# Output buffer freed at the head of a GpSimd step, and row loads awaited two units later on a semaphore for each parity

## The chip, the cores and the metric

The kernel runs on one core of a Trainium2 chip. The metric is device time in microseconds (us) of one execution; the number compared is the median over several runs. Lower is better. The core's engines are TensorE (PE), VectorE (DVE), ScalarE (ACT), GpSimd (POOL) and SyncE (SP), which work in parallel and are tied together by semaphores; 16 DMA engines move data between HBM and the core's memory.

## What is computed

Eight blocks of 100 tokens of width 512 go through an attention-like layer (keys, gate and values are the same context `c`) and then through a top-1 mixture of 16 experts. Cut to what matters:

```python
x = x + einsum(gelu(layernorm(x) @ c.T) * (layernorm(x) @ c.T), c)     # per block, c is 722 x 512
h = layernorm(x).reshape(800, 512)
logits = h @ router_w                     # 512 x 16
assign = argmax(logits); w = sigmoid(logits[assign])
out = (gelu(h @ w1[assign] + b1[assign]) @ w2[assign] + b2[assign]) * w
x = x + out
```

Each expert has `w1` (512 x 1024) and `w2` (1024 x 512) in f32, so 4 MB; all 16 are read once.

## The kernel before

**First part, to about 120 us.** For each of the eight blocks PE, ACT and DVE compute the first layer, the routing and each token's rank in its expert. Rows (token, gate, mean, inverse root, output row number) are scattered by GpSimd into a table `rows` in HBM, sorted by expert.

**Second part, in units.** A unit is up to 32 tokens of one expert. A unit's rows are laid as 128 partitions x 132 values (4 quarters of the token's width). Units 0 to 3 are head units of experts 0 to 3; all further ones stand in the order of the experts, and with the inputs drawn there are 32 units in all (the trace has 32 scatters at L860). By a count of the tokens that these inputs send to each expert, units 8 to 11 belong to expert 3, unit 12 to expert 4, units 28 to 30 to expert 14 and unit 31 to expert 15.

For unit j the engines do:

- PE: `first_layer(j)` (L385, into `p_h`), the transpose of the next unit's tokens (L404), `second_layer(j-1)` (L396, into `p_y`). `second_layer(j)` waits until `finish(j-1)` has read `p_y` (`s_yo`).
- DVE: transpose and bias of the hidden units (L682, L688), normalization of the tokens two units ahead (`next_tokens(j+2)`, L672, which waits on `s_land` for the rows to have landed), bias of the residual (L694), and `finish(j-1)` (L705), which writes one half of the double buffer `y_out`. `finish(j)` waits on `s_y_free >= j + 1`.
- ACT: the gelu (L491).
- GpSimd: `scatter_unit(j, r)`, with r the parity of j: it waits until scatter j-2, which read the same half of `y_out`, has landed (`s_done[r]`), adds one to `s_y_free`, copies the row numbers (L856), waits for `finish(j)` (`s_yo`) and issues the indirect DMA to `out` (L860). While rows are still to be loaded, GpSimd also issues two row loads per unit (`load_unit`, L213, 66 KB each; each first reads its column from a table into a register, L212).
- SP: `load_half` (L232), 1 MB pieces of the experts' weights, four to an expert. There are four slots of weights; experts 4 to 15 (48 pieces) go into a slot when the expert four before has done its last `first_layer` (`s_hp`, for w1) or `second_layer` (`s_y`, for w2). The pieces are issued in order.

**What sets the order on GpSimd.** All is written out by hand, each engine's instructions run in program order. Units 8 to 11 are loaded beside `scatter_unit(2)` and `(3)`. Then a loop L888 of `loading` rounds (4 here) takes two units a round: `scatter_unit(4)` to `(11)`, with the loads of units 12 to 27. A loop L895 loads the units left over (28 to 31), after which the last wait on `s_ld` stands, and a loop L899 runs `scatter_unit(12)` to `(31)` with no loads. All row loads from unit 8 on count on the one semaphore `s_ld`; GpSimd tells DVE of landed rows by `s_land`. The step of a unit in L888 is: issue two loads, wait `s_next` and `s_done[r]`, free `y_out`, scatter, then wait on `s_ld` for the loads issued in this same step.

Of the kernel before, what the change touches and what calls it, by code (L numbers as in the profile page):

```python
# [35 lines left out]
SLOTS = 4  # L36
# [3 lines left out]
OWN = 8  # L40
NEAR = 12
# [47 lines left out]
def build(nc, x, ctx_main, ctx_rest, ctxT_a, ctxT_b, router, w1, b1, w2, b2, consts, out):  # L89
# [3 lines left out]
    with ExitStack() as stack:  # L93
# [3 lines left out]
        def sem(name):  # L97
            return stack.enter_context(nc.semaphore(name))

        def sems(name, n):  # L100
            return [sem(f"{name}{i}") for i in range(n)]
# [75 lines left out]
        s_x, s_ctx = sems("s_x_in", 3), sems("s_ctx", 2)  # L177
        s_w1, s_w2 = ([sems(f"{n}_{i}_", 2) for i in range(SLOTS)] for n in ("s_w1", "s_w2"))
        s_b2, s_b2_rest, s_row = sem("s_b2"), sem("s_b2_rest"), sems("s_row", RB)
        s_own, s_ld, s_land, s_blank = sems("s_own", OWN - SLOTS), sem("s_ld"), sem("s_land"), sem("s_blank")  # L180

        s_x1ps, s_tps, s_lgps = sems("s_x1ps", 2), sem("s_tps"), sem("s_lgps")
        s_xnps, s_att, s_rkps, s_cntps = sem("s_xnps"), sem("s_att"), sem("s_rkps"), sem("s_cntps")
# [16 lines left out]
        s_next = sem("s_next")  # L200
        s_prep, s_yo, s_out_at, s_y_free = (sem(n) for n in ("s_prep", "s_yo", "s_out_at", "s_y_free"))
# [5 lines left out]
        def units(eng):  # L207
            return eng.value_load(ends[0:1, E - 1:E], min_val=SLOTS + E, max_val=MAXU)

        def load_unit(eng, j, signal):  # L210
            at = bass.ds(j, 1) if not isinstance(j, int) else slice(j, j + 1)
            col = eng.value_load(colof[0:1, at], min_val=0, max_val=E * PER - 1)  # L212
            eng.dma_start(xr[:, at, :].rearrange("p o d -> p (o d)"),  # L213
                          rows[bass.ds(col * U, U), :].rearrange("t (q d) -> q t d", q=Q)).then_inc(signal, 16)
# [571 lines left out]
        def _(pool):  # L786
            def apart():
                pool.sem_inc(s_apart_p, 1)
# [55 lines left out]
                                             nothing[:, :], None, bounds_check=last_row, oob_is_err=False  # L844
                                             ).then_inc(s_pad[i], 16)

            def scatter_unit(j, r, before):
                at = slice(j, j + 1) if isinstance(j, int) else bass.ds(j, 1)
                mine = head if isinstance(j, int) and j < SLOTS else xr
                pool.wait_ge(s_next, j + 1)  # L850
                if before is not None:
                    pool.wait_ge(s_done[r], before)
                apart()
                if before is not None:
                    pool.sem_inc(s_y_free, 1)  # L855
                nc.gpsimd.tensor_copy(out_at[r][:, :], mine[:, at, DQ + 3].bitcast(U32)).then_inc(s_out_at, 1)  # L856
                pool.wait_ge(s_out_at, j + 1)
                pool.wait_ge(s_yo, j + 3)
                apart()
                nc.gpsimd.indirect_dma_start(out_q, bass.IndirectOffsetOnAxis(ap=out_at[r][:, :], axis=0),  # L860
                                             y_out[:, r, :], None, bounds_check=last_out, oob_is_err=False
                                             ).then_inc(s_done[r], 16)

            scatter_unit(0, 0, None)
            pool.wait_ge(s_blank, 1)
            for i in range(RB):
# [5 lines left out]
            for j in range(SLOTS + 1, OWN):  # L872
                load_unit(pool, j, s_own[j - SLOTS])
            scatter_unit(1, 1, None)
            for i in range(1, PADS):
                pool.wait_ge(s_pad[i], 16)
                apart()

            for j in range(2, SLOTS):
                for k in range(2):  # L880
                    load_unit(pool, OWN + 2 * (j - 2) + k, s_ld)
                scatter_unit(j, j % 2, 16 * (j // 2))
                pool.wait_ge(s_ld, 32 * (j - 1))
                pool.sem_inc(s_land, 2)
            n = units(pool)
            less = pool.value_load(n_less[0:1, 0:1], min_val=SLOTS + E - NEAR - 1, max_val=MAXU - NEAR - 1)
            loading, pairs = pool.snap(less // 4), pool.snap((less + (NEAR - 2)) // 2)
            with pool.Fori(0, loading) as i:  # L888
                for r in range(2):
                    for k in range(2):  # L890
                        load_unit(pool, 4 * i + (NEAR + 2 * r + k), s_ld)
                    scatter_unit(2 * i + (SLOTS + r), r, 16 * i + 32)
                    pool.wait_ge(s_ld, 64 * i + (16 * (NEAR - OWN) + 32 * r + 32))
                    pool.sem_inc(s_land, 2)
            with pool.Fori(4 * loading + NEAR, n) as j:  # L895
                load_unit(pool, j, s_ld)
            pool.wait_ge(s_ld, 16 * less + 16 * (NEAR + 1 - OWN))
            pool.sem_inc(s_land, 4)
            with pool.Fori(loading, pairs) as i:  # L899
                for r in range(2):  # L900
# [36 lines left out]
```

## Time and profile before

| | us |
|---|---|
| median of 3 runs (lowest to highest) | 328.78 (328.36 to 329.91) |
| the profiled execution, its own time | 326.27 |
| its span in the profile | 324.6 |
| granted TensorE clock, mean over the span | 0.911 |
| busy: PE / PE weight load / DVE / POOL / ACT | 253.4 / 179.8 / 113.0 / 89.0 / 32.4 |

The numbers of the trace are those of the profiled execution: 1.67 us of its time lie outside the span, and it is 2.5 us below the median of the runs. A row of the timeline is start, duration, engine, line, operation, and in brackets how long the engine had been idle and what ended that. The weights and activations have come from one queue that SP issues (q1), the row loads and scatters from one that GpSimd issues (q0).

### The profile page before, as it was taken

To read this page: it belongs to the slowest core of one execution; us is meant where nothing else is said; L and a number is where in the kernel's file an instruction comes from. 1 tells how busy PE (TensorE), PEld (TensorE's weight loads), DVE (VectorE), ACT (ScalarE), POOL (GpSimd) and SP (SyncE) were. 2 spreads that over 40 slices of the span, in tenths; PEclk is the share of its full clock that TensorE was granted. 3 is DMA by queue.
4 is the path that set the end of the run, shared out by engine and by line. 5 is a ranking of instruction groups with operands and counts; after the bars stand their busy time and mean duration, and the time that the engine had idled before them with its cause. 6 is when DMAs were issued, how large, how long until landed. Compare 5 with 4: busy or idle time off the path is not lost. (4 is left out here: it accounts for less than half of the span.)

```text
span 324.6 us, 9969 instructions
## 1 busy us (share of the span) xinstructions
PE 253.4 (78%) x3763; PEld 179.8 (55%) x3764; DVE 113.0 (35%) x385; ACT 32.4 (10%) x76; POOL 89.0 (27%) x141
## 2 busy tenths in 40 slices
PE   1899999999999898784663747840197999899982
PEld 0868867867867456553431544520175766566762
DVE  2134444444442663242210222220043344344430
ACT  0311111112011021010000000000010111011110
POOL 1002312312341353533330234413022122221222
PEclk9999999999999959995979569895579999999998
DMA  7999899999999998753999806599759999999700
GB/s 252 377 357 361 287 371 343 385 378 342 418 381 309 420 418 327 121 182 138 291 403 361 305 25 236 176 364 375 245 209 424 424 423 426 420 421 424 289 16 14
DMA packets 21437, 100.93 MB, mean 311 GB/s; under 512 B 4942, under 2 KB 6882, under 8 KB 12200
## 3 DMA queue, kind: packets, MB, share of 16 engines
q1 hardware_dynamic: 16680, 93.81, 77.0%
q0 software_dynamic: 4592, 6.56, 6.6%
q8 instruction: 14, 0.23, 0.3%
q10 hardware_dynamic: 144, 0.27, 0.2%
q14 instruction: 7, 0.06, 0.1%
HBM read 95.89 MB, written 5.14 MB: 311 GB/s over the span
## 5 line engine op out<-in xcount | busy, mean ns | idle before, releaser
L396 PE MATMUL bank<-W,area 128*32 128x128 f32 x2048 | 76.2, 295 | 41.3 <-DVE area L705 38.5
L396 PEld LDWEIGHTS bank<-W,area 128*32 128x32 f32 x2048 | 61.9, 118 | 51.5 <-DVE area L705 40.3
L385 PE MATMUL bank<-W,area 128*32 128x256 f32 x1024 | 69.0, 409 | 14.9 <-issue 14.5
L385 PEld LDWEIGHTS bank<-W,area 128*32 128x32 f32 x1024 | 37.1, 117 | 36.8 <-issue 24.6
L860 POOL DMA_INDIRECT out<-area,out_at x32 | 32.4, 1012 | 72.1 <-DVE area L705 57.8
L316 PEld LDWEIGHTS bank<-xnT,area 128*128 128x128 f32 (+1 forms) x384 | 44.7, 194 | 4.7 <-issue 4.7
L323 PE MATMUL bank<-area,hidT 128*100 128x512 f32 (+1 forms) x96 | 46.8, 601 | 0.0
L316 PE MATMUL bank<-xnT,area 128*128 128x100 f32 (+1 forms) x384 | 45.1, 280 | 1.4 <-issue 1.4
L705 DVE SCALAR_TENSOR_TENSOR area<-bank,area 128x128 f32 (+1 forms) x28 | 9.8, 351 | 86.7 <-POOLq L855 65.8
L213 POOL DMA_DIRECT2D area<-rows x27 | 19.2, 711 | 53.5 <-issue 53.5
L491 ACT ACTIVATE area<-area 128x256 f32<-128x256 f32 x32 | 13.4, 417 | 187.6 <-PE bank L396 177.5
L682 DVE STREAM_TRANSPOSE area<-bank 128x256 f32<-128x256 f32 x32 | 14.4, 449 | 39.6 <-PE bank L385 28.4
L804 POOL DMA_INDIRECT rows<-row,pos x8 | 8.7, 1082 | 49.6 <-DVE pos L569 32.6
L323 PEld LDWEIGHTS bank<-area,hidT 128*100 128x100 f32 (+1 forms) x96 | 13.7, 167 | 10.0 <-issue 10.0
L525 DVE TENSOR_TENSOR hidT<-hidT,bank 128x300 f32<-128x300 f32 x16 | 7.4, 464 | 19.5 <-ACT hidT L463 19.5
L688 DVE TENSOR_TENSOR area<-area,b1s 128x256 f32<-128x256 f32 x32 | 13.6, 424 | 0.2 <-DVE area L682 0.2
L404 PEld LDWEIGHTS bank<-con,area 128*128 128x128 f32 x33 | 4.7, 142 | 14.7 <-issue 14.6
L672 DVE TENSOR_SCALAR area<-area 128x128 f32 (+1 forms) x28 | 9.8, 350 | 7.7 <-DMA area<-rows 3.9
L463 ACT ACTIVATE hidT<-bank 128x300 f32<-128x300 f32 x16 | 6.8, 422 | 56.4 <-PE bank L316 56.4
L792 POOL TENSOR_TENSOR rs_x<-ve_x,con 100x1 f32<-100x1 f32 x8 | 4.5, 558 | 25.9 <-DVE ve_x L511 25.9
L404 PE MATMUL bank<-con,area 128*128 128x128 f32 x33 | 11.2, 341 | 0.1
L792 POOL TENSOR_TENSOR row<-ve_t,con 100x4 f32<-100x4 f32 x8 | 8.4, 1049 | 9.2 <-DVE ve_t L511 9.0
(95 smaller groups left out, 146.0 us busy)
## 6 DMA issues: line engine op xcount, KB each, us to landing
W<-in_w SPq DMA_DIRECT2D x64, 1024.0 KB, 11.9
area<-in_ctx_main SPq DMA_DIRECT2D x8, 1280.0 KB
area<-in_ctxT_a SPq DMA_DIRECT2D x8, 768.0 KB, 8.8
area<-in_ctxT_b SPq DMA_DIRECT2D x8, 676.0 KB, 8.0
area<-rows POOLq DMA_DIRECT2D x27, 66.0 KB, 7.1
xs<-in_x SPq DMA_DIRECT2D x8, 200.0 KB
area<-in_ctx_rest SPq DMA_DIRECT2D x8, 160.0 KB
xs<-in_b SPq DMA_DIRECT2D x4, 192.0 KB
```

Source lines behind the costliest of these rows:

```text
L213: eng.dma_start(xr[:, at, :].rearrange("p o d -> p (o d)"), rows[bass.ds(col * U, U), :].rearrange("t (q d) -> q t d", q=Q)).then_inc(sign ...
L316: last = nc.tensor.matmul((p_xa, p_xb)[part][0:n, T * c:T * c + T], ctxTs[b % 2][part][:, k, P * c:P * c + n], xnT[:, k, :], start=(k == 0 ...
L323: last = nc.tensor.matmul(p_att[0:T, :], hidT[0:CW[c], c, :], cxs[b % 2][0:CW[c], c, :], start=(c == 0), stop=(c == SC - 1))
L385: last = nc.tensor.matmul(p_h[U * q:U * q + U, 0:FQ], curT[:, U * k:U * k + U], mine, start=(k == 0), stop=(k == KD - 1), tile_position=(0 ...
L396: last = nc.tensor.matmul(p_y[U * q:U * q + U, 0:DQ], hT[:, U * c:U * c + U], W2[:, slot, c, DQ * q:DQ * q + DQ], start=(c == 0), stop=(c ...
L404: nc.tensor.transpose(p_blk[:, 0:P], cur, ident).then_inc(s_blk, 1)
L491: nc.scalar.activation(hT, h_pre, ACT.Gelu).then_inc(s_act, 1)
L672: nc.vector.tensor_scalar(cur, mine[:, 0:DQ], mine[:, DQ + 1:DQ + 2], mine[:, DQ + 2:DQ + 3], ALU.subtract, ALU.mult).then_inc(s_next, 1)
L682: nc.vector.transpose(h_pre, p_h[:, 0:FQ]).then_inc(s_hT, 1)
L688: nc.vector.tensor_tensor(view, view, bias.unsqueeze(3).to_broadcast([P, 2, Q, U]), ALU.add).then_inc(s_hb, 1)
L792: nc.gpsimd.tensor_tensor(rs, ve, neg_half.to_broadcast(list(rs.shape)), ALU.pow).then_inc(s_rs, 1)
L860: nc.gpsimd.indirect_dma_start(out_q, bass.IndirectOffsetOnAxis(ap=out_at[r][:, :], axis=0), y_out[:, r, :], None, bounds_check=last_out, ...
```

## The change

Line numbers in the text are those of the kernel before. In `scatter_unit`, the wait for scatter j-2 and the increment of `s_y_free` now come first; then an optional hook runs, then the wait on `s_next`, the copy, the wait on `s_yo` and the scatter, as before. The hook is `load_two`: it waits for the pair of loads issued two units ago (the one of the same parity, on its own semaphore `s_ld[r]`), adds 2 to `s_land`, and issues the next two loads. The loads left over count on a third semaphore, `s_left`. After them GpSimd waits for both parities and then for `s_left`, before `scatter_unit(12)`.

```diff
-            def scatter_unit(j, r, before):
+            def scatter_unit(j, r, before, ahead=None):
                 at = slice(j, j + 1) if isinstance(j, int) else bass.ds(j, 1)
                 mine = head if isinstance(j, int) and j < SLOTS else xr
-                pool.wait_ge(s_next, j + 1)
                 if before is not None:
                     pool.wait_ge(s_done[r], before)
+                    apart()
+                    pool.sem_inc(s_y_free, 1)
+                if ahead is not None:
+                    ahead()
+                pool.wait_ge(s_next, j + 1)
                 apart()
-                if before is not None:
-                    pool.sem_inc(s_y_free, 1)
                 nc.gpsimd.tensor_copy(out_at[r][:, :], mine[:, at, DQ + 3].bitcast(U32)).then_inc(s_out_at, 1)
...
-            for j in range(2, SLOTS):
+            def load_two(j, r, landed):
+                if landed is not None:
+                    pool.wait_ge(s_ld[r], landed)
+                    pool.sem_inc(s_land, 2)
                 for k in range(2):
-                    load_unit(pool, OWN + 2 * (j - 2) + k, s_ld)
-                scatter_unit(j, j % 2, 16 * (j // 2))
-                pool.wait_ge(s_ld, 32 * (j - 1))
-                pool.sem_inc(s_land, 2)
+                    load_unit(pool, j + k, s_ld[r])
+
+            for r in range(2):
+                scatter_unit(2 + r, r, 16, lambda: load_two(OWN + 2 * r, r, None))
...
             with pool.Fori(0, loading) as i:
                 for r in range(2):
-                    for k in range(2):
-                        load_unit(pool, 4 * i + (NEAR + 2 * r + k), s_ld)
-                    scatter_unit(2 * i + (SLOTS + r), r, 16 * i + 32)
-                    pool.wait_ge(s_ld, 64 * i + (16 * (NEAR - OWN) + 32 * r + 32))
-                    pool.sem_inc(s_land, 2)
+                    scatter_unit(2 * i + (SLOTS + r), r, 16 * i + 32,
+                                 lambda: load_two(4 * i + (NEAR + 2 * r), r, 32 * i + 32))
             with pool.Fori(4 * loading + NEAR, n) as j:
-                load_unit(pool, j, s_ld)
-            pool.wait_ge(s_ld, 16 * less + 16 * (NEAR + 1 - OWN))
+                load_unit(pool, j, s_left)
+            for r in range(2):
+                pool.wait_ge(s_ld[r], 32 * loading + 32)
+                pool.sem_inc(s_land, 2)
+            pool.wait_ge(s_left, 16 * (less % 4) + 16)
             pool.sem_inc(s_land, 4)
```

GpSimd's instructions in the loop L888, from the scatter of an even unit to the first row load of the odd unit behind it, before (ISA and REGISTER_ALU rows are register work; `s_ld` stands before the next load):

```order
L860 DMA out<-area,out_at0 3200x128 [waits s_yo]
L893 ISA
L212 ISA [waits s_ld]
L212 TENSOR_LOAD colof
L212 ISA x2
L213 ISA
L213 REGISTER_ALU
L213 DMA area<-rows 128x1x132
```

and in the changed kernel, with its own line numbers (`s_done1` is of the scatter before this one, `s_ld1` of the pair issued two units ago):

```order
L863 DMA out<-area,out_at0 3200x128 [waits s_yo]
L213 ISA [waits s_done1,s_ld1]
L213 TENSOR_LOAD colof
L213 ISA x2
L214 ISA
L214 REGISTER_ALU
L214 DMA area<-rows 128x1x132
```

The wait for the pair just issued is gone from there; the wait for the scatter, with the freeing of `y_out` behind it, has moved up past the loads.

The second place is the end of the loads, from the last of the row loads left over to the first scatter behind them, before:

```order
L213 DMA area<-rows 128x1x132
L895 REGISTER_ALU
L895 COMPARE_AND_BRANCH
L897 ISA
L899 UNCONDITIONAL_BRANCH [waits s_ld]
L899 ISA
L852 ISA [waits s_next]
L856 ISA [waits s_done0]
L856 COPY out_at0<-area 128x1
```

and in the changed kernel:

```order
L214 DMA area<-rows 128x1x132
L899 REGISTER_ALU
L899 COMPARE_AND_BRANCH
L902 ISA
L904 ISA [waits s_ld0,s_ld1]
L906 UNCONDITIONAL_BRANCH [waits s_left]
L906 ISA
L857 ISA [waits s_done0]
L859 ISA [waits s_next]
L859 COPY out_at0<-area 128x1
```

There GpSimd still stands until every load has landed before it frees `y_out` for unit 12; three waits stand in place of one.

## Rows read from the trace of the kernel before

**Rows 1.** Windows, two stages: stretch and length, busy us of each engine, PE clock, DMA share, GB/s.

```profile
142.00:212.00 70.00, 44.54 (x806) 30.02 (x798) 16.09 (x49) 3.34 (x8) 22.35 (x33) 0.80 0.70 248
...
235.00:320.00 85.00, 76.66 (x1765) 54.77 (x1757) 35.73 (x106) 7.52 (x18) 22.39 (x38) 0.97 0.81 332
```

**Rows 2.** Waits, 140 to 240 us: engine, line, waited for: us in total, times, longest.

```profile
DVE area L705 <- POOLq L855: 65.8, 9, 20.7
POOL area L213 <- issue: 48.6, 21, 7.0
```

**Rows 3.** Timeline of POOL: scatters of units 7, 8, 9 and what stands between.

```profile
180.71 1.05 POOL L860 DMA_INDIRECT out<-area,out_at  x1 [1.16 <-DVE area L705]
188.24 0.74 POOL L213 DMA_DIRECT2D area<-rows  x1 [6.48 <-issue]
...
191.70 1.04 POOL L860 DMA_INDIRECT out<-area,out_at  x1 [1.23 <-DVE area L705]
194.39 0.75 POOL L213 DMA_DIRECT2D area<-rows  x1 [1.64 <-issue]
195.77 0.68 POOL L213 DMA_DIRECT2D area<-rows  x1 [0.63 <-issue]
196.45 0.20 POOL L856 COPY out_at<-area 128x1 uint32 x1
197.81 1.05 POOL L860 DMA_INDIRECT out<-area,out_at  x1 [1.16 <-DVE area L705]
```

**Rows 4.** Timeline of DVE: `finish(4)` and `finish(12)`.

```profile
149.89 0.35 DVE L705 SCALAR_TENSOR_TENSOR area<-bank,area 128x128 f32<-128x128 f32 x1 [7.12 <-POOLq L855]
...
233.66 0.35 DVE L705 SCALAR_TENSOR_TENSOR area<-bank,area 128x128 f32 x1 [20.75 <-POOLq L855]
```

**Rows 5.** Timeline of POOL: scatter of unit 3, and the loop's first load.

```profile
142.05 1.13 POOL L860 DMA_INDIRECT out<-area,out_at  x1 [0.92 <-POOL out_at L856]
148.15 0.74 POOL L213 DMA_DIRECT2D area<-rows  x1 [4.97 <-issue]
```

**Rows 6.** Timeline of POOL: scatter 11, loads left over, first copy behind them; last scatter.

```profile
211.06 1.05 POOL L860 DMA_INDIRECT out<-area,out_at  x1 [1.18 <-DVE area L705]
219.12 0.74 POOL L213 DMA_DIRECT2D area<-rows  x1 [7.01 <-issue]
220.87 0.68 POOL L213 DMA_DIRECT2D area<-rows  x1 [1.01 <-issue]
...
224.40 0.68 POOL L213 DMA_DIRECT2D area<-rows  x1 [1.10 <-issue]
233.28 0.18 POOL L856 COPY out_at<-area 128x1 uint32 x1 [8.20 <-DMA area<-rows]
...
320.38 0.98 POOL L860 DMA_INDIRECT out<-area,out_at  x1 [1.92 <-DVEq L783]
```

**Rows 7.** Page, DMA issues: name, queue, count, KB each, median us from issue to landing.

```profile
W<-in_w SPq DMA_DIRECT2D x64, 1024.0 KB, 11.9
...
area<-rows POOLq DMA_DIRECT2D x27, 66.0 KB, 7.1
```

**Rows 8.** Timeline of POOL: scatter 14, and the copy that waited for its landing.

```profile
244.77 0.98 POOL L860 DMA_INDIRECT out<-area,out_at  x1 [3.76 <-DVE area L705]
...
250.69 0.18 POOL L856 COPY out_at<-area 128x1 uint32 x1 [0.81 <-DMA out<-area,out_at]
```

**Rows 9.** DMA queues, 170 to 174 us: packets, MB, share of 16 engines.

```profile
q1 hardware_dynamic: 157, 1.15, 93.0%
q0 software_dynamic: 140, 0.13, 12.4%
```

**Rows 10.** The same, 250 to 270 us.

```profile
q1 hardware_dynamic: 1131, 8.28, 98.7%
```

**Rows 11.** Timeline of PE: second layer of unit 13, and first layer of unit 28.

```profile
234.07 3.64 PE L396 MATMUL bank<-W,area 128*32 128x128 f32 x64 [19.00 <-DVE area L705]
...
298.30 1.93 PE L385 MATMUL bank<-W,area 128*32 128x256 f32 x32 [0.51 <-issue]
```

More of the change, by code:

```diff
@@ L179, in build @@
         s_b2, s_b2_rest, s_row = sem("s_b2"), sem("s_b2_rest"), sems("s_row", RB)
-        s_own, s_ld, s_land, s_blank = sems("s_own", OWN - SLOTS), sem("s_ld"), sem("s_land"), sem("s_blank")
+        s_own, s_land, s_blank = sems("s_own", OWN - SLOTS), sem("s_land"), sem("s_blank")
+        s_ld, s_left = sems("s_ld", 2), sem("s_left")
         s_x1ps, s_tps, s_lgps = sems("s_x1ps", 2), sem("s_tps"), sem("s_lgps")
```

## The prediction, made before the changed kernel had run

> **What bounds the kernel now.** I read the windows first. From 142 to 212 us PE is busy 44.5 of 70 us and the DMA engines 70%, so neither of the two resources that the units need is the bound there; from 235 us on PE is busy 76.7 of 85 us at nearly full clock, and that part is bound by compute [rows 1]. The waits say who holds the first stretch: DVE stood 65.8 us, nine times, at `finish` (L705), and what ended it was GpSimd's increment of `s_y_free` at L855; GpSimd itself stood 48.6 us ahead of its row loads [rows 2]. Nine times are units 4 to 12. The timeline shows why: after scatter 7 ended at 181.76, GpSimd stood 6.48 us before its next load, though between two loads of a pair the gap is 0.63 us [rows 3]. What it stood for is the wait on `s_ld`, that is, for the pair of loads it had just issued; behind that wait stand the next pair, and only then the freeing of `y_out`. So each unit's `finish`, and with it PE's second layer of the next unit, hangs on the landing of loads whose rows are used several units later. The distance of two scatters is 10.99 us (180.71 to 191.70) while weights fill the DMA engines and 6.11 us (191.70 to 197.81) when they don't [rows 3]. The longest of the nine waits is 20.75 us, at `finish(12)` [rows 4]: there GpSimd issues the four loads left over and waits for them all [rows 6].
>
> **Step 1, entry to the loop.** Before, scatter 3 ended at 143.18 and the loop's first load started at 148.15, 4.97 us later [rows 5]. The change takes away the landing; left are the reads of two counts and of the loads' column. A load behind loop bookkeeping starts 1.01 us after the one before [rows 6], and a further register read and load costs 0.63 [rows 3]; I take 1.0 + 2 x 0.63 = 2.3 us (between 1.0 and 4.97). First load at 145.5, then 0.74 + 0.63 + 0.68 for the pair, 0.20 for the copy, 0.92 until the scatter starts [rows 3, 5]: scatter 4 at 148.7. `finish(4)`, before at 149.89 [rows 4], comes near 144.7, before its unit's loads and not behind them.
>
> **Step 2, units 5 to 11.** GpSimd's own work per unit doesn't shrink: gap 1.0, loads 0.75 + 0.63 + 0.68, copy 0.20, 0.92, scatter 1.05, together 5.23 us [rows 3, 5, 6]. That is the floor. It is above 4.6 us, the distance of two units in the last stage (233.66 to 320.38 for 19 units) [rows 4, 6], so GpSimd's instruction stream becomes the pace. The nearest measured value is 6.11 us, the unit in which loads landed fast [rows 3]; it still holds a little landing (gap 1.64 against 1.0) and a late `finish` (1.16 against 0.92). Against the floor speak the two waits that remain. The scatter of two units ago must have landed: with a latency L, two units last at least L + 5.23. Scatter 14 ended at 245.75 and released the copy at 250.69 beside full weight traffic, L = 4.9 [rows 8], which gives 5.1 us a unit. The pair of two units ago took about 7.9 us beside weights (issued by 179.3, landed by 187.2, 1.0 before the next load) [rows 3], and two units less the issue time give it over 8. Both fit just below 6, and both at once in one queue will cost something; I take 6.0 us. Seven units: scatter 11 at 148.7 + 42.0 = 190.7, before 211.06 [rows 6], so 20.4 us less.
>
> **Step 3, the loads left over.** Before: 7.01 us until the first of four, mostly landing; after, 1.0. From the first load's start to the last one's end 5.96 us, then 8.20 until all had landed [rows 6]; neither is touched. `y_out` is free for unit 12 at 191.75 + 1.0 + 5.96 + 8.20 = 206.9, before 233.28: 26.4 us less. A stall of some 13 us at `finish(12)` stays; the change doesn't reach it.
>
> **Step 4, units 12 to 31.** They run as before, bound by PE: there `finish` waited for PE, not for GpSimd (all nine waits on GpSimd lie ahead). Moving the wait on `s_next` behind the freeing costs nothing, since next tokens are prepared two units ahead. The sem operations are as many as before, bar two. But this holds only if the weights keep up, since the stream of 48 pieces of 1.05 MB (50.3 MB) has to fit into less time. Beside row loads q1 moves 1.15 MB in 4 us, 0.29 MB/us [rows 9]; without them 8.28 in 20, 0.414 [rows 10]. From 144, after scatter 3, to 206.9 at 0.29 that is 18.2 MB. The tightest point is w1 of expert 14, whole after 44.0 MB: 206.9 + 25.8 / 0.414 = 269.2; it is needed at 298.30 - 26.4 = 271.9 [rows 11]. That fits by 2.7 us, by some 5 if q1 runs at its full rate in the tenth or fifth of each unit in which the other queue rests. So the weights hide behind compute, narrowly, and a gain beyond some 30 to 33 us isn't to be had.
>
> **Sum.** 326.27 - 26.4 = 299.9 us for the profiled execution. The median of the runs stood 2.5 us above it; I carry that over: **302.4 us**. With the floor of 5.23 in step 2 it is 5.4 less, with a landing of 7.1 [rows 7] in place of 8.2 another 1.1: 295.9.
>
> **Rivals.**
> (A) *The queue becomes the pace.* Scatters now stand behind two loads of the same step and ahead of two of the next. If a scatter waits until the pair before it is through (7.9 less the 2.2 us between, 5.7) and then takes its own 4.9, L is 10.6 and a unit (10.6 + 5.23) / 2 = 7.9 us. For it: loads are slow beside weights, and the weights will now be moving all the time. Against it: after scatter 7 everything issued was landed 5.5 us later (181.76 to 187.2) [rows 3]. In between, L = 9.4, 7.3 us a unit: 7 x 1.3 = 9.1 us more, 311.5; at 7.9, 315.7.
> (B) *The weights become the bound.* If q1 moves only 0.24 MB/us in the stage, 15.1 MB by 206.9, w1 of expert 14 comes at 276.7, 4.8 us late: 307.2. The same page of the Trainium skill, section "Queues, rings and completion order", says that each DMA engine takes turns between its queues packet by packet, so that small packets displace large ones. Rows 9 and 10 agree (0.414 falls to 0.29), and by the rule a denser row queue would push the rate down no further, since turns are already taken.
> (C) *PE's clock.* The second layer after the long stall took 3.64 us, at the lower clock (1.2 GHz), where a first layer at 2.4 GHz takes 1.93 [rows 11]. If the clock stays down because PE rests a part of each unit, a unit takes 3.64 + 2 x 1.93 + 0.5 = 8.0 us: 14 us more, 316.4. Against: 0.80 granted in the worse stage already [rows 1].
> (D) *Slower.* The wait for the scatter now stands ahead of the loads and no longer beside them. If L grows because every step feeds the queue before the last one has drained, that wait takes the place of the old one. Break-even: 148.7 + 7U + 16.2 = 233.28, U = 9.8, so L = 14.3; slower by over 0.5% from L = 14.8. At the old pace of 10.99 it would be 148.7 + 76.9 + 16.2 = 241.8, 8.5 more than 233.28: 337.3. L would have to be three times the 4.9 of rows 8.
> (E) *It doesn't do what it says*: the landing of row loads isn't what GpSimd stands for, its pause of 6.48 us belongs to issuing the loads and stays, and with it the distance of 10.99 us and the time of 328.8. Against: the first load of the next pair had a gap of 6.48 in one unit and 1.64 in the next with the same instructions [rows 3]; a load lands 7.1 us after its issue in the median [rows 7]; and PE's second layer started 0.06 us after `finish(12)` had ended and had stood 19.00 us for it [rows 4, 11]. A rule speaks for this rival: the Trainium skill, page "DMA: Bandwidth & Descriptors", section "Anatomy of one DMA — SWDGE (gpsimd) path", fits a GpSimd DMA with 2.0 us plus its bytes at 436 GB/s. By that a row load would land in an estimated 2.2 us, about when the scatter behind it has been issued, the loop would hold hardly a wait to remove, and the gain there would be near zero. The trace disagrees, with 7.1 us, where weights fill the same DMA engines, and it decides.
>
> **How the numbers follow.** Forecast 0.62 (its own range 296 to 306), A 0.23, B 0.04, C 0.05, D 0.04, E 0.02. The forecast, A, B and C are all faster by over 0.5%, which is about what a measurement of this kernel can tell from no change; D is slower, E the same: 0.94, 0.02, 0.04. The range goes from the floor of step 2, at 295.5, to 314, through most of A; outside lie D, E, most of C and the end of A.
>
> **What the profile would show.** Right: DVE's waits at `finish` on GpSimd shrink from 65.8 us to some 20 to 30, nearly half of it in one wait of 12 to 15 us at unit 12; scatters 5 to 11 about 6 us apart; copy 12 near 207; the last scatter near 294; q1 above the 248 GB/s of the first window, with hardly a pause. Step 2 wrong: distances of 7 us and more, GpSimd idle ahead of its first load of each pair, ended by a DMA. Step 4 wrong: PE idle ahead of first layers after 207 us while the DMA share is full. The forecast would be wrong at the root if the waits at L705 stayed and another releaser's name stood by them.

## The result and the profile after

| | before | changed |
|---|---|---|
| median (lowest to highest), us | 329.35 (328.36 to 335.05), 4 runs | 303.52 (303.01 to 314.25), 4 runs |
| profiled execution, own time | 326.27 | 303.48 |
| its span | 324.6 | 301.8 |
| granted TensorE clock | 0.911 | 0.942 |

The ratio is 0.922, 95% interval 0.918 to 0.926. One run of each kernel (335.05 and 314.25) was disturbed and isn't in the ratio. The forecast was 302.4 with a range of 295.5 to 314.

Windows of the changed kernel (stretch and length, busy us of PE, PE weight load, DVE, ACT, POOL, then PE clock, DMA share, GB/s):

```profile
142.00:191.00 49.00, 36.27 (x742) 24.70 (x733) 14.54 (x44) 3.33 (x8) 19.61 (x29) 0.90 1.00 343
191.00:212.00 21.00, 4.47 (x109) 3.24 (x108) 2.01 (x6) 0.42 (x1) 5.62 (x9) 0.68 1.02 354
212.00:297.00 85.00, 76.19 (x1773) 55.39 (x1765) 35.73 (x106) 7.50 (x18) 22.63 (x39) 0.98 0.83 341
```

Against [rows 1], the stage of the row loads now has its DMA engines busy without a pause (1.00 for 0.70) and PE busy 74% of it for 64%. The last stage is the same 85 us with the same work, only 23 us earlier. Waits of the changed kernel, 140 to 220 us:

```profile
DVE area L706 <- POOLq L854: 25.0, 4, 17.6
POOL area L214 <- issue: 23.3, 21, 3.5
...
PE bank L386 <- issue: 11.9, 7, 4.2
```

DVE's wait for the buffer fell from 65.8 us in nine pieces to 25.0 in four [rows 2], and GpSimd's pauses ahead of its loads from 48.6 to 23.3. Of the 25.0, 17.6 is one piece, at `finish(12)`. The timeline of POOL, from scatter 3 to scatter 8 and from scatter 11 to the end (L863 is the scatter, L214 a row load, L859 the copy):

```profile
141.79 1.04 POOL L863 DMA_INDIRECT out<-area,out_at  x1 [0.91 <-POOL out_at L859]
144.65 0.74 POOL L214 DMA_DIRECT2D area<-rows  x1 [1.82 <-issue]
...
148.01 1.04 POOL L863 DMA_INDIRECT out<-area,out_at  x1 [0.96 <-POOL out_at L859]
150.06 0.74 POOL L214 DMA_DIRECT2D area<-rows  x1 [1.01 <-issue]
...
153.29 1.04 POOL L863 DMA_INDIRECT out<-area,out_at  x1 [0.97 <-POOL out_at L859]
157.83 0.74 POOL L214 DMA_DIRECT2D area<-rows  x1 [3.50 <-issue]
...
161.05 1.04 POOL L863 DMA_INDIRECT out<-area,out_at  x1 [0.96 <-DMA out<-area,out_at]
...
170.73 1.05 POOL L863 DMA_INDIRECT out<-area,out_at  x1 [5.86 <-DVE area L706]
...
175.99 1.04 POOL L863 DMA_INDIRECT out<-area,out_at  x1 [0.97 <-POOL out_at L859]
...
194.88 1.04 POOL L863 DMA_INDIRECT out<-area,out_at  x1 [0.98 <-POOL out_at L859]
196.58 0.74 POOL L214 DMA_DIRECT2D area<-rows  x1 [0.66 <-issue]
...
201.84 0.68 POOL L214 DMA_DIRECT2D area<-rows  x1 [1.10 <-issue]
210.92 0.18 POOL L859 COPY out_at<-area 128x1 uint32 x1 [8.41 <-DMA area<-rows]
...
296.94 0.98 POOL L863 DMA_INDIRECT out<-area,out_at  x1 [1.93 <-DVEq L784]
```

Scatters 4 to 11 take 46.87 us (148.01 to 194.88) where they took 59.69 (151.37 to 211.06, the latter in [rows 6]): 6.70 us a unit for 8.53. Three of the steps (5.26 to 5.61 us) are close to the 5.23 us of GpSimd's own instructions. The others show two things that stand in the way, and they are different. At 157.83 the load waits 3.50 us and at 191.52 another one 2.65; the trace gives 6.2 us in two places for row loads that waited for a scatter's landing (who waited for the scatters, 140 to 215 us):

```profile
  POOL area L214: 6.2, 2
```

And at 170.73 the scatter stood 5.86 us for DVE's `finish(7)`, which was late because PE was. Timeline of PE, first layers of units 7 and 8, and the second layer after the long stall:

```profile
151.38 3.24 PE L386 MATMUL bank<-W,area 128*32 128x256 f32 x32 [4.20 <-issue]
...
157.63 1.06 PE L386 MATMUL bank<-W,area 128*32 128x256 f32 x13 [0.77 <-issue]
162.76 2.77 PE L386 MATMUL bank<-W,area 128*32 128x256 f32 x19 [4.08 <-issue]
...
211.54 3.64 PE L397 MATMUL bank<-W,area 128*32 128x128 f32 x64 [16.07 <-DVE area L706]
```

PE stood twice for some 4 us with nothing in the profile that it waited for, once in the midst of a first layer. Before, the second of these was 2.79 us; at the first, PE had just stood 4.78 us for `finish(4)`, and no such pause shows. Behind each pause PE ran slower for a while: from 162 to 170 us the mean granted clock was 0.64 of 2.4 GHz.

```profile
162.00:170.00 8.00, 7.24 (x112) 4.64 (x115) 2.02 (x6) 0.42 (x1) 1.71 (x4) 0.64 1.04 322
```

### The profile page after: what moved, and what is told of

It reads as the page before. It is cut to its first block and busy times, and to the rows that moved or that the text cites. A ratio compares the mean times of both kernels' runs of the same rounds, so it can differ in the third digit from the quotient of the medians.

```text
span 301.8 us, 9996 instructions
## 1 busy us (share of the span) xinstructions
PE 245.1 (81%) x3763; PEld 175.8 (58%) x3764; DVE 112.9 (37%) x385; ACT 32.4 (11%) x76; POOL 89.1 (30%) x141
## 5 line engine op out<-in xcount | busy, mean ns | idle before, releaser
L397 PE MATMUL bank<-W,area 128*32 128x128 f32 x2048 | 71.0, 282 | 21.0 <-DVE area L706 18.1
L386 PE MATMUL bank<-W,area 128*32 128x256 f32 x1024 | 68.1, 399 | 19.8 <-issue 19.7
L397 PEld LDWEIGHTS bank<-W,area 128*32 128x32 f32 x2048 | 58.6, 113 | 29.2 <-DVE area L706 18.8
L386 PEld LDWEIGHTS bank<-W,area 128*32 128x32 f32 x1024 | 37.6, 114 | 39.9 <-issue 27.2
L863 POOL DMA_INDIRECT out<-area,out_at x32 | 32.3, 1010 | 69.8 <-DVE area L706 54.1
L214 POOL DMA_DIRECT2D area<-rows x27 | 19.2, 710 | 28.2 <-issue 28.2
L793 POOL TENSOR_TENSOR rs_x<-ve_x,con 100x1 f32<-100x1 f32 x8 | 4.5, 557 | 25.9 <-DVE ve_x L512 25.9
L859 POOL COPY out_at<-area 128x1 uint32 x28 | 5.8, 207 | 20.3 <-DMA area<-rows 8.4
```

Of the source, the lines that this page charges most:

```text
L214: eng.dma_start(xr[:, at, :].rearrange("p o d -> p (o d)"), rows[bass.ds(col * U, U), :].rearrange("t (q d) -> q t d", q=Q)).then_inc(sign ...
L386: last = nc.tensor.matmul(p_h[U * q:U * q + U, 0:FQ], curT[:, U * k:U * k + U], mine, start=(k == 0), stop=(k == KD - 1), tile_position=(0 ...
L397: last = nc.tensor.matmul(p_y[U * q:U * q + U, 0:DQ], hT[:, U * c:U * c + U], W2[:, slot, c, DQ * q:DQ * q + DQ], start=(c == 0), stop=(c ...
L793: nc.gpsimd.tensor_tensor(rs, ve, neg_half.to_broadcast(list(rs.shape)), ALU.pow).then_inc(s_rs, 1)
```

## The experiments

The experiments ran in three groups, each on one chip with the kernel before beside them, whose median was 323.04 us in the first group (experiments 1 to 4), 327.92 in the second (5 to 8) and 327.83 in the third (9 to 12). So ratios are compared, not times. Experiments 8 and 9 are the changed kernel itself, once more. Where an edit is a small one of the changed kernel, the diff is against that.

### 1. The early freeing alone

```diff
-                pool.wait_ge(s_next, j + 1)
                 if before is not None:
                     pool.wait_ge(s_done[r], before)
+                    apart()
+                    pool.sem_inc(s_y_free, 1)
+                if ahead is not None:
+                    ahead()
+                pool.wait_ge(s_next, j + 1)
                 apart()
-                if before is not None:
-                    pool.sem_inc(s_y_free, 1)
...
-                    for k in range(2):
-                        load_unit(pool, 4 * i + (NEAR + 2 * r + k), s_ld)
-                    scatter_unit(2 * i + (SLOTS + r), r, 16 * i + 32)
+                    scatter_unit(2 * i + (SLOTS + r), r, 16 * i + 32, lambda: load_two(4 * i + (NEAR + 2 * r)))
                     pool.wait_ge(s_ld, 64 * i + (16 * (NEAR - OWN) + 32 * r + 32))
                     pool.sem_inc(s_land, 2)
```

> Half of the change alone: y_out is freed at the head of the step, but GpSimd still waits at its end for the two loads of the same step. Theory (the landing wait is the price, since it stands ahead of the next freeing wherever in the step that is): the step stays loads 2.8 + copy 0.2 + 0.92 + scatter 1.05 + landing, 11 us beside weights; only the finish that was late by 0.24 us a unit and the time of one pair's issue at unit 4 are saved: 2 to 3 us off, 326 us, ratio 0.99. Rival (the late freeing was what held PE): most of the 26 us go, 305 to 310 us.

Ratio 0.987 (0.981 to 0.993), 4 us. Its waits, 140 to 240 us:

```profile
DVE area L705 <- POOLq L853: 63.3, 9, 17.7
POOL area L213 <- issue: 50.7, 21, 7.2
```

Nine waits of 63.3 us in all are nearly the 65.8 of the kernel before [rows 2]. The increment that the next `finish` needs stands behind the landing wait at the end of the step before, wherever in its own step it stands.

### 2 and 10. The late wait alone

```diff
-                if before is not None:
-                    pool.wait_ge(s_done[r], before)
-                    apart()
-                    pool.sem_inc(s_y_free, 1)
                 if ahead is not None:
                     ahead()
                 pool.wait_ge(s_next, j + 1)
+                if before is not None:
+                    pool.wait_ge(s_done[r], before)
                 apart()
+                if before is not None:
+                    pool.sem_inc(s_y_free, 1)
```

> The other half alone: loads are awaited two units later by parity, but y_out is freed behind the pair's issue and the wait for next tokens, as before. Theory: the landing wait is gone, so nearly the whole gain stays; the finish comes 2.8 us later in each step, which costs 0.2 to 0.3 us a unit and more where PE is late: 305 to 308 us. Rival (freeing first is what counts): near 325 us.

Ratio 0.922 (0.911 to 0.932): as large a gain as the whole change has. Run again beside the changed kernel, to tell the two apart:

> Late wait only, the buffer freed behind the loads as before, now beside the changed kernel on one chip. Theory (the late wait carries the whole gain; the early freeing exposes the scatter's landing in front of the loads for what it gives PE): within 0.5% of the changed kernel. Rival (freeing first is worth a part of its own): 2 to 4 us slower than the changed kernel.

> The changed kernel again, the measure for the three others of this comparison. Expected: 0.922 to 0.926 of the kernel before.

0.926 (0.921 to 0.932) against 0.930 (0.923 to 0.938) for the changed kernel: the early freeing gives nothing that these runs can tell. The trace of experiment 2 shows why, in timeline rows of POOL:

```profile
150.81 1.04 POOL L863 DMA_INDIRECT out<-area,out_at  x1 [1.45 <-DVE area L706]
152.67 0.74 POOL L214 DMA_DIRECT2D area<-rows  x1 [0.81 <-issue]
...
158.02 1.04 POOL L863 DMA_INDIRECT out<-area,out_at  x1 [3.08 <-DMA area<-rows]
159.31 0.74 POOL L214 DMA_DIRECT2D area<-rows  x1 [0.25 <-issue]
```

With the wait for the scatter behind the loads, loads start 0.25 and 0.81 us after the scatter, for 1.01 and 3.50 in the changed kernel: the scatter's landing is hidden behind the issue of two loads. In exchange `finish` comes later, and the scatter stands for it: 1.17 to 1.45 us in five of the seven steps, where it was some 0.97. (The 3.08 and an 8.41 at unit 7 have PE's pauses in them: both `finish` instructions had stood for PE.) Over the seven steps the pauses ahead of the first load sum to 4.7 us for 11.7, those ahead of the second to 5.9 for 4.8, and those ahead of the scatter to 17.7 for 11.7, so scatters 4 to 11 took 46.9 us here too (145.49 to 192.40). The gap of 0.25 also bounds the new wait on `s_ld[r]` there: the pair of two units ago had landed. Once it had not: at 183.50 the load stood 2.12 us, and the trace names a row load as what it waited for.

### 3. The pair of one unit ago awaited, in place of two

```diff
-                    pool.wait_ge(s_ld[r], landed)
+                    pool.wait_ge(s_ld[1 - r], landed)
...
-                                 lambda: load_two(4 * i + (NEAR + 2 * r), r, 32 * i + 32))
+                                 lambda: load_two(4 * i + (NEAR + 2 * r), r, 32 * i + (32 + 32 * r)))
...
```

The counts at the entry to the loop and behind it are changed to match.

> As the changed kernel, but GpSimd waits for the pair issued one unit ago, not two. A pair lands about 8 us after its issue beside weights. From the end of a pair's issue to this wait there are 2.2 us (copy, scatter). Theory: the freeing has already been done, but the loads wait about 5 to 6 us each unit, so the step is about 11 us beside weights as before and 6 elsewhere: 318 to 326 us. Wait, the buffer is free a step earlier, so DVE and PE run one step ahead, which is worth one step at the end at most (0 to 5 us of this range). Rival (a distance of one is enough): 303 to 306 us.

Ratio 0.970 (0.961 to 0.979). On the scale of the kernel before that is 319 us, in the range of the theory. Timeline of POOL:

```profile
169.07 1.04 POOL L863 DMA_INDIRECT out<-area,out_at  x1 [0.96 <-POOL out_at L859]
177.87 0.74 POOL L214 DMA_DIRECT2D area<-rows  x1 [7.76 <-issue]
...
181.07 1.04 POOL L863 DMA_INDIRECT out<-area,out_at  x1 [0.96 <-POOL out_at L859]
```

The wait of 7.76 us ahead of the load is as long as before (6.48 in [rows 3]), and the step is 12.0 us. Scatters 4 to 11 took 66.2 us (147.49 to 213.68), 6.5 more than before. The 3% come from elsewhere: from entering the loop without a landing wait (scatter 4 at 147.5 for 151.4), and from the loads left over (scatters 11 to 12: 14.3 us, for 24.0 before). "One unit ago" sounds like a distance of a unit and is none: between the end of a pair's issue and this wait stand only a copy and a scatter, 2.2 us, as in the kernel before, where the wait stands at the end of the step. What has changed is that the freeing has passed the wait. So the experiment shows two things. A wait placed there is too near for a landing of some 8 us. And the freeing alone isn't the hold: the scatters no longer stood for `finish` (0.96 us behind the copy), and still the pace was not better, since the loads, and the scatter behind them, stand in GpSimd's own order behind the landing.

### 4. The last wait moved behind scatters 12 and 13

```diff
-            for r in range(2):
-                pool.wait_ge(s_ld[r], 32 * loading + 32)
-                pool.sem_inc(s_land, 2)
+            def landed(r):
+                pool.wait_ge(s_ld[r], 32 * loading + 32)
+                pool.sem_inc(s_land, 2)
+            for r in range(2):
+                scatter_unit(pool.snap(2 * loading + (SLOTS + r)), r, 16 * loading + 32, lambda: landed(r))
             pool.wait_ge(s_left, 16 * (less % 4) + 16)
             pool.sem_inc(s_land, 4)
-            with pool.Fori(loading, pairs) as i:
+            with pool.Fori(loading + 1, pairs) as i:
```

> The changed kernel, and the wait for the loads left over moved behind scatters 12 and 13 (the two pairs of loads before are awaited one in each of these steps). Theory: the wait of 17.6 us at finish(12) falls to 2 to 6 us; units 12 on start 12 to 15 us earlier; the weights then bound the end, since the last piece landed at 283.3 and was needed at 293: gain 6 to 10 us, 294 to 298 us, with PE idle ahead of first layers in the last stage. Rival (the weights aren't near): the full 12 to 15, 289 to 291 us. Rival (no gain, the stall returns two units later): 302 to 304 us.

Ratio 0.915 (0.906 to 0.923), beside 0.922 for experiment 2 on the same chip: 2 us by the ratios, not the 6 to 10 expected, and not clear of the intervals. Timelines: POOL from the first load left over to copy 12; DVE at `finish(12)`; PE in the first layer of unit 28:

```profile
200.79 0.74 POOL L214 DMA_DIRECT2D area<-rows  x1 [0.65 <-issue]
...
206.89 0.18 POOL L859 COPY out_at<-area 128x1 uint32 x1 [0.18 <-issue]
```

```profile
206.95 0.35 DVE L706 SCALAR_TENSOR_TENSOR area<-bank,area 128x128 f32 x1 [9.15 <-POOLq L854]
```

```profile
269.08 1.07 PE L386 MATMUL bank<-W,area 128*32 128x256 f32 x16 [0.61 <-DMA W<-in_w]
271.54 1.07 PE L386 MATMUL bank<-W,area 128*32 128x256 f32 x16 [1.39 <-DMA W<-in_w]
```

I had overlooked that the freeing for unit 12 still stands behind the issue of the four loads, 6 us; so 9.15 of 17.56 us stayed. And weights are now late: PE stood 2.0 us for them, at expert 14, the place that the prediction had named as the tightest. In the two profiled executions the part that the edit touches does show the gain expected: from scatter 11 to the last one 92.1 us (199.09 to 291.17) for the 98.6 of experiment 2 (192.40 to 291.01). But scatter 4 came at 151.04 there and at 145.49 in experiment 2, in a stretch that differs only by the late freeing, and why isn't known. So the 2 us of the ratios are what is measured, and that the edit is worth no more isn't shown.

### 5 and 6. Both kernels with an eighth of the later weights' bytes

Of the 48 later pieces only 16 of 128 partitions are loaded, so twelve of the 16 experts compute with stale weights in the rest; all else is the same.

```diff
-                    load_half(W1[:, s], first, s_w1[s], 0)
+                    load_half(W1[0:16, s], first[0:16], s_w1[s], 0)
```

(the same for the other three pieces)

> The kernel before, with only 16 of 128 partitions loaded in each of the 48 later weight pieces (an eighth of the bytes in as many transfers; these experts compute with stale weights elsewhere). Theory (row loads are slow because weights fill the DMA engines): the waits ahead of row loads fall from 6.5 to 2 us, scatters 4 to 11 come 6.2 us apart (59.7 us before, 43 here), the stall at finish(12) falls from 20.8 to about 10: about 26 us less than the kernel before. Rival (the landing is a fixed cost of GpSimd's DMAs): distances as before, no more than 2 us less. On PE the first pass through its loop, ahead of first layers, should lose its idle 3 to 4 us if the code is fetched over the same engines.

> The changed kernel with the same cut in the weights. Theory: both waits are covered, scatters 4 to 11 come 5.3 to 5.6 us apart (GpSimd's own instructions), 39 us in all against 46.9; PE's idle of 4.2 and 4.1 us ahead of two first layers falls below 1.5; the stall at finish(12) is 12 us (loads' issue 6 and landing 3.5 to 4): 13 us less than the changed kernel, and about 12 less than the small-weight kernel before, so under half of the gain is left. Rival (the gain doesn't rest on weight traffic): 25 us between the two.

> The changed kernel itself, once more, as the measure for the three others on the same chip. Expected: ratio 0.922 as measured before.

Ratios: 0.949 (0.941 to 0.956) for the kernel before with the cut, 0.894 (0.886 to 0.901) for the changed one with it, 0.926 (0.918 to 0.934) for the changed one without. So of the change's 24 us (0.074 of 327.9) 18 are left (0.055): I had expected 12. The kernel before got 17 us faster by the cut, not the 26 expected. The stall at `finish(12)` was 15.45 us in it (10 expected) and 12.46 in the changed one (12 expected). The windows from 142 to 212 us, kernel before with the cut, then changed kernel with it:

```profile
142.00:212.00 70.00, 45.40 (x841) 30.73 (x829) 16.81 (x51) 3.75 (x9) 23.13 (x34) 0.88 0.39 64
```

```profile
142.00:212.00 70.00, 49.23 (x1022) 35.14 (x1014) 20.72 (x63) 4.51 (x11) 27.04 (x42) 0.88 0.56 77
```

The cut took away seven eighths of the weights' bytes, but not of the engines' time: their share is still 0.39 and 0.56 at 64 and 77 GB/s. The weights' queue alone fell from 62.3% to 25.9% in the kernel before and from 90.4% to 37.1% in the changed one. So the cut separates less than was meant, and the share of weight traffic in a landing stays open. What it does show: with less traffic the loads of the kernel before wait less, though not all of them; the pauses ahead of the first loads of units 5 to 11 sum to 19.3 us for 27.7. Timeline of POOL of the kernel before with the cut:

```profile
164.96 0.74 POOL L213 DMA_DIRECT2D area<-rows  x1 [5.50 <-issue]
...
171.00 0.74 POOL L213 DMA_DIRECT2D area<-rows  x1 [1.55 <-issue]
```

Scatters 4 to 11 came in 51.4 us for 59.7, and in the changed kernel in 40.6 for 46.9, 5.80 us a unit against the floor of 5.23. The part on PE came out nearly as expected. First layers of units 7 and 8, changed kernel with the cut, and unit 8, kernel before with the cut:

```profile
149.88 1.93 PE L386 MATMUL bank<-W,area 128*32 128x256 f32 x32 [1.75 <-issue]
...
157.62 1.49 PE L386 MATMUL bank<-W,area 128*32 128x256 f32 x19 [1.33 <-issue]
```

```profile
163.21 1.49 PE L385 MATMUL bank<-W,area 128*32 128x256 f32 x19 [1.14 <-issue]
```

4.20 and 4.08 us became 1.75 and 1.33 (below 1.5 expected), and 2.79 became 1.14. In the nine other traces with the changed entry to the loop and full traffic, the two pauses are 3.22 to 4.27 and 3.31 to 4.90 us, so the shrinking is clear of their scatter. It isn't the whole account, though: in the changed kernel with the cut PE also stood 2.85 us within a second layer, at 166.44, without a named cause, which no trace with full traffic has.

### 7 and 11. One more round in the loop, no load left over

```diff
-            loading, pairs = pool.snap(less // 4), ...
+            loading, pairs = pool.snap((less + 1) // 4), ...
...
-            with pool.Fori(4 * loading + NEAR, n) as j:
-                load_unit(pool, j, s_left)
+            with pool.If(n > 4 * loading + NEAR):
+                with pool.Fori(4 * loading + NEAR, n) as j:
+                    load_unit(pool, j, s_left)
```

and behind it the two steps of experiment 4, then one `sem_inc(s_left, 16)` and a wait for `16 * ((less + 1) % 4) + 16`.

> The changed kernel with one more round in the loop (all 20 loads in pairs, none left over here), and the last two pairs awaited in steps 14 and 15. Theory: no long stall at finish(12) or later, units 12 and 13 come at the pace of the loop, units from 14 on 3 to 6 us earlier than with the wait moved only; but the weights bound the end already there (PE waited 2 us for them at unit 28), so the last scatter gains at most 0 to 2 us on that one: ratio 0.905 to 0.915, with several us of waits on weights ahead of first layers. Rival (compute still bounds): 5 us more than the wait moved only, ratio 0.90.

> One more round in the loop and no long wait at its end, beside the changed kernel on one chip. The weights end the gain: 7 to 10 us less than the changed kernel, not the 14 or 15 that the stall at finish(12) is long.

Ratios 0.902 (0.893 to 0.910) and 0.903 (0.896 to 0.910), beside 0.926 and 0.930 of the changed kernel on the same chips: 8 to 9 us faster than it. It beats both kernels; its interval overlaps that of experiment 4, run on another chip. The 17.56 us stall is gone, but 5.1 us of waits for weights have come in, by the waits of experiment 11 from 212 to 300 us:

```profile
PE bank L386 <- DMA W<-in_w: 5.1, 6, 1.4
```

The rest of the difference is that the stall was never worth its whole length. Scatters 11 and 12, in the changed kernel on the same chip (experiment 9), then in experiment 11:

```profile
194.25 1.05 POOL L863 DMA_INDIRECT out<-area,out_at  x1 [0.98 <-POOL out_at L859]
212.20 1.04 POOL L863 DMA_INDIRECT out<-area,out_at  x1 [1.39 <-issue]
```

```profile
196.54 1.05 POOL L863 DMA_INDIRECT out<-area,out_at  x1 [0.98 <-POOL out_at L859]
203.01 1.04 POOL L863 DMA_INDIRECT out<-area,out_at  x1 [0.98 <-POOL out_at L859]
```

Without the stall the step still takes 6.47 us, for 17.95 with it: 11.5 us are won there. From scatter 12 to the last one it is 88.2 us (203.01 to 291.24) for 84.2 (212.20 to 296.41), so 4.0 us come back. That leaves 7.5 in the profiled executions, of the 9 of the ratios.

### 12. The same with the buffer freed behind the loads

This is experiment 11 with the diff of experiment 2.

> The same with the buffer freed behind the loads: the scatter's landing is then covered by the pair's issue (2.8 us). Theory: GpSimd's steps lose up to 3 us in two or three units, the finish comes 2.8 us later in each; with the weights as the bound at the end neither shows: within 1% of the version before it. Rival: 2 to 4 us faster, the fastest of all.

Median 299.68 us of six runs from 294.65 to 301.37, a spread that leaves no ratio with an interval. Its two fastest runs (294.65 and 295.79) lie within the 293.30 to 298.93 of experiment 11, whose median is 297.34: it isn't shown to be either faster or slower. PE stood 7.1 us for weights in it, which is in line with the theory and no more than that.

## Why the prediction was right, step by step

**What bounds the kernel.** The pauses of GpSimd are landing waits and they set the pace through `s_y_free`. Shown: of the two halves of the change, the late wait alone carries 0.922, the early freeing 0.987; with the pair of one unit ago awaited, 2.2 us behind its issue, the wait is as long as before. One point is put too narrowly: the pace isn't held through `s_y_free` alone. In experiment 3 the freeing had passed the landing wait and the step was no shorter, because GpSimd's own loads and scatters stood behind that wait.

Rival E is out: with the wait moved the pauses went, so they didn't belong to issuing. By the fit of the Trainium skill (page "DMA: Bandwidth & Descriptors", section "Anatomy of one DMA — SWDGE (gpsimd) path") a row load would land in an estimated 2.2 us; the trace of the changed kernel disagrees, with 8.1 us in the median, and it decides.

**Step 1** put scatter 4 at 148.7; it came at 148.01. The gap to the loop's first load was 1.82 us, forecast 2.3, and `finish(4)` came at 143.62, forecast 144.7.

**Step 2** is where the sum was off: 6.0 us a unit forecast, 6.70 measured, 46.87 us for 42.0, so 4.9 us too little. The floor was right (5.26 to 5.61 in three of the seven steps), its additions weren't. Gaps ahead of the first load were 11.7 us over seven steps where the floor counts 7.0: the latency L of a scatter was taken as 4.9, from a stage without row loads [rows 8]. Here scatter 4 ended at 149.05, and the load behind its landing started at 157.83; with the floor's gap of 1.0 taken off, that is up to 7.8 us. The 4.9 was also one sample: where copies of the changed kernel waited for a landing in its last stage, L was 5.2 to 5.7. Rival A held in this for single steps, at some three quarters of its 10.6, but not for the pace. The other term was not in the sum at all: 4.9 us at unit 7 (5.86 less 0.92), GpSimd standing for a `finish` that PE had made late. PE's pause of 4.08 us was behind that, and the lower clock after it: the 19 matmuls behind the pause and the second layer took 2.77 and 2.83 us, where 1.49 and 1.95 were seen at the higher level (experiment 6), 2.2 us in all. I had read PE as having room (4.6 us a unit), from the last stage, in which no pause without a named cause is longer than 1.7 us.

**Step 3** forecast 1.0, 5.96 and 8.20 us; measured 0.66, 5.94 and 8.41. Copy 12 came at 210.92 for 206.9, by the error of step 2. The stall that stays was forecast as some 13 us and was 17.56. From scatter 11 to copy 12 it is 16.0 us, as forecast (16.2), but DVE, freed earlier in its step, was ready for `finish(12)` 1.3 us ahead of scatter 11 (at 193.57), where before it was ready 1.9 behind it.

**Step 4** held: from copy 12 to the last scatter 86.0 us (210.92 to 296.94) for 87.1 before [rows 6]. The weights stayed hidden, no wait of PE for them, and by more than forecast: q1 moved 21.3 MB from 144 us to copy 12, 0.318 MB/us for the 0.29 of [rows 9], and had moved 43.9 MB by 269 us, while the first layer of unit 28 started at 274.99. By that w1 of expert 14 was there some 6 us early, an estimate from the queue's bytes, where the forecast had 2.7. That they were near was right too: in experiments 4, 7, 11 and 12, which start the last stage earlier, PE waits for them, and experiments 7 and 11 end 32 us below the kernel before, within the 30 to 33 that the forecast had named as the most to be had.

**The sum.** 303.48 us for the profiled execution, forecast 299.9: 4.0 too little at copy 12, 1.1 too much behind it, and 0.6 that the span's end lay later behind the last scatter. The 2.5 us that I carried over from the median of before covered most of that by luck: the changed kernel's median stood 0.04 us above its profiled execution. The forecast of 302.4 against 303.52 is better than its steps. The range has a slip: its lower end, given as 295.5 and as the floor of step 2, is 295.9 by its own sum, and holds the shorter landing of step 3 too.

**Rivals.** C is out as the pace: the clock was 0.90 from 142 to 191 us, for 0.80 from 142 to 212 before. It held in one step, the only one above 8.0 us (9.68, scatters 6 to 7), where PE's pause of 4.08 us was followed by a clock of 0.64. B is out for the changed kernel, with 0.318 MB/us for its 0.24; late weights came up only in the versions that start the last stage earlier. D is out: L would have had to be 14.3.

## What to carry to other kernels

A wait placed in a step behind everything else still stands ahead of the next step's first instruction: ask which later step needs what has been awaited, and wait there, with one semaphore for each transfer that can be in flight. The distance has to cover the landing under load, measured beside the real traffic, and it is counted in time from the transfer's issue to the wait, not in steps. Here 2.2 us did nothing for a landing of about 8; a whole step more, so some 8 us in all, took the wait away but for one of 2.12 us. Where a buffer's freeing is moved ahead of other work, look at the wait that it takes along: here it exposed a scatter's landing, and the two came out even. After such a gain look for the next bound before removing the next stall: of 17.6 us of stall only 8 to 9 could be won, since the step takes 6.5 us without the stall too and the weights took back 4.

## What the runs showed of the hardware that I had not expected

- **PE stood without a named cause early in its unit loop, and longer where the DMA engines were full.** Ahead of or within the same two first layers it stood 4.20 and 4.08 us in the changed kernel, 1.75 and 1.33 with the weights' bytes cut to an eighth; in the kernel before, 2.79 and 1.14. That it fetches code over the same DMA engines is argued, not shown. The dependence on traffic is shown for these pauses, one trace for each kernel with the cut; the 2.85 us at another place with the cut is not explained.
- **A scatter landed later where row loads shared its queue.** It landed 4.9 us after its issue with scatters alone in the queue [rows 8] (5.2 to 5.7 in the changed kernel's last stage), and up to 7.3 and 7.8 where two row loads stood in each step, the weights' queue running in both. The two are from different stages, so that the row loads are the reason is argued, not shown.
- **Fewer bytes aren't fewer busy engines.** With pieces of 16 partitions all queues together moved 64 and 77 GB/s and still held the DMA engines 39% and 56% of the time, where with full pieces it was 248 GB/s with 70% in the kernel before and 343 GB/s with 100% in the changed one (142 to 191 us).
